# Four chained sequence layers on one core: layer-norm sums over chunks made on VectorE, the value bias of layer 3 moved behind the attention, and other load and product orders on both sides of attention 2

## The reference

```python
# layer 0: recurrent mixing with a token shift, then a small feed-forward part
xn = layernorm(x) * w + b;  dx = shifted(xn) - xn;  five mixes of xn and dx -> key, decay, value, receptance, gate
scan over the sequence (16 x 16 state per head), group norm, gate, @ Wo.T, + x
xn = layernorm(x) * w + b;  x = x + sigmoid(.. @ Wr.T) * (relu(.. @ Wk.T)**2 @ Wv.T)
# layer 1: cross attention of x on layernorm(context), 16 heads;  x = x + tanh(gate) * (attn @ Wo.T)
# layer 2: grouped cross attention, 32 heads on 8 key/value heads, bias on q, k, v, output;  x = layernorm(attn @ Wo + bo + x)
# layer 3 (x: context, latents: output of layer 2)
h = concatenate([x, latents], axis=1)
q = (latents @ q_w + q_b);  kv = (h @ kv_w + kv_b);  k, v = kv[..., 0], kv[..., 1]
attn = softmax(where(mask, q k^T / DH, -inf));  attn_out = attn @ v
attn_out = attn_out @ out_w + out_b + latents
out = rmsnorm(attn_out, postnorm_w);  out = gelu(out @ mlp_w1 + mlp_b1) @ mlp_w2 + mlp_b2;  return out + latents
```

## Time and profile before

| | us |
|---|---|
| median of three runs (lowest, highest) | 6026.17 (6018.28, 6046.16) |
| the profiled execution's own time | 6028.71 |
| its span in the profile | 6026.9 |
| TensorE busy | 5352.1 (89%) |
| VectorE busy | 3558.0 (59%) |
| ScalarE busy | 2765.7 (46%) |
| GpSimd busy | 1470.6 (24%) |

### The profile page before, as it was taken

How to read it: one execution, slowest core, us unless ns; L and a number is a source line. 1 busy time by engine, 2 the same in 40 slices (tenths; PEclk the granted TensorE clock), 3 DMA queues, 4 the chain that set the end, 5 groups by cost and what they waited for, 6 DMA issues and landing times. The chain is left out here.

```text
span 6026.9 us, 69068 instructions
## 1 busy us (share of the span) xinstructions
PE 5352.1 (89%) x26050; PEld 1878.7 (31%) x26050; DVE 3558.0 (59%) x4608; ACT 2765.7 (46%) x5261; POOL 1470.6 (24%) x708
## 2 busy tenths in 40 slices
PE   6987999999697999996788888886879999997999
PEld 2333333434233233322222222222323333322444
DVE  4548777877342777750588888881137777761010
ACT  2423333333122466662377777773215666663111
POOL 0004333334000466660000000000005666662000
PEclk8988999999799899998799999998979999998999
DMA  3233333333221322313111111112234232302000
GB/s 107 96 103 103 96 84 87 91 95 88 82 70 38 80 63 62 73 31 110 42 28 30 32 29 28 30 22 85 75 77 80 53 71 58 66 26 98 21 21 14
DMA packets 459769, 383.48 MB, mean 64 GB/s; under 512 B 169809, under 2 KB 359094, under 8 KB 458764
## 3 DMA queue, kind: packets, MB, share of 16 engines
q1 hardware_dynamic: 459428, 379.00, 23.4%
HBM read 242.83 MB, written 135.14 MB: 63 GB/s over the span
## 5 line engine op out<-in xcount | busy, mean ns | idle before, releaser
L2174 DVE TENSOR_REDUCE att_part<-att_scores 128x1 f32<-128x423 f32 (+1 forms) x2304 | 1190.2, 579 | 425.9 <-PE att_scores L2021 424.6
L2138 ACT ACTIVATE att_prob<-att_scores 128x512 f32<-128x512 f32 (+1 forms) x1920 | 993.5, 601 | 549.1 <-PE att_scores L2033 548.6
L2157 POOL TENSOR_TENSOR att_acc<-att_acc,att_prob 128x1024 f32<-128x1024 f32 (+1 forms) x416 | 984.7, 2367 | 441.3 <-ACT att_prob L2138 439.2
L2481 DVE TENSOR_REDUCE att_part<-att_scores 128x2 f32<-128x802 f32 x1024 | 964.6, 988 | 161.9 <-PE att_scores L2385 155.7
L2467 ACT ACTIVATE att_prob<-att_scores 128x512 f32<-128x512 f32 (+1 forms) x1664 | 861.4, 602 | 252.2 <-PE att_scores L2399 250.4
L2021 PE MATMUL att_scores<-att_k,att_q 97*128 97x423 f16 (+1 forms) x2304 | 816.5, 358 | 84.4 <-DMA att_q<-in_c_q 60.4
L2033 PE MATMUL att_scores<-att_q,att_k 98*128 98x512 f16 (+1 forms) x1920 | 721.5, 383 | 13.6 <-ACT att_prob L2138 13.4
L1264 POOL TENSOR_TENSOR scan_z<-scan_r,scan_states 128x512 f32<-128x512 f32 x256 | 410.1, 1602 | 1107.8 <-DVE scan_states L1297 1092.7
L2157 POOL TENSOR_TENSOR att_acc<-att_prob 128x1024 f32<-128x1024 f32 x32 | 75.6, 2364 | 2443.2 <-ACT att_prob L2138 2443.2
L2399 PE MATMUL att_scores<-att_q,att_k 49*128 49x512 f16 (+1 forms) x1664 | 471.7, 390 | 110.1 <-ACT att_prob L2467 109.9
L2044 PE MATMUL att_sums<-att_prob,att_v 128*32 128x512 f32 (+1 forms) x3840 | 510.9, 604 | 0.0
(11 more groups left out here) (294 smaller groups left out, 6103.3 us busy)
## 6 DMA issues: line engine op xcount, KB each, us to landing
v<-scan_val SPq DMA_DIRECT2D x96, 256.0 KB, 2.3
att_v<-v SPq DMA_DIRECT2D x32, 768.0 KB
att_spread<-recips SPq DMA_DIRECT2D x64, 256.0 KB
mix_plane<-in_mask SPq DMA_DIRECT2D x16, 800.5 KB, 6.6
att_k<-k1hi SPq DMA_DIRECT2D x32, 400.2 KB
att_k<-k3hi SPq DMA_DIRECT2D x32, 400.2 KB
scan_x<-in_ctx_t SPq DMA_DIRECT2D x12, 1024.0 KB, 8.9
o<-att_out SPq DMA_DIRECT2D x32, 256.0 KB, 2.1
```

The source lines that it names most:

```text
L2138: nc.scalar.activation(prob[g % NP][0:kw(kt), h, :], scores2[0:kw(kt), n % RING2, :], ACT.Exp).then_inc(exped, 1)
L2157: nc.gpsimd.tensor_tensor(acc[s % 2][0:kw(kt)], so_far[0:kw(kt), 0:PH, :], prob[g % NP][0:kw(kt), 0:PH, :], ALU.add).then_inc(padded, 1)
L2174: nc.vector.reduce_max(part[q % 2][:, hc, piece:piece + 1], scores1[:, bank["piece", p], 0:PIECE], AX.X).then_inc(reduced, 1)
L2481: nc.vector.reduce_max(part[q % 2][:, :, ec, piece], scores1[:, bank["unit", p], :, 0:PIECE], AX.X).then_inc(reduced, 1)
```

## The change

Six edits. In the four norm stages VectorE first adds the four chunks of x, or of `sq`, into `sq[:, 0]` (two adds, of 128 x 1024 and of 128 x 512), and the group on TensorE has one matmul instead of four. In "mlp" there is only the second moment. In "mix" VectorE adds up x when it comes to "mean" in its own order, and the squares behind that step's mask reductions.

```diff
@@ mix; ffn and mid2 the same, behind the residual add and behind the centring @@
                     if what == "mean":
-                        pe.wait_ge(xloaded[b % 2], 16 * (b // 2 + 1))
-                        group([(k["mean"][:], x[b % 2][:, c, :]) for c in range(C)])
+                        pe.wait_ge(totalled, 2 * b + 1)
+                        group([(k["mean"][:], sq[:, 0, :])])
                     elif what == "std":
-                        pe.wait_ge(squared, b + 1)
-                        group([(k["mean"][:], sq[:, c, :]) for c in range(C)])
+                        pe.wait_ge(totalled, 2 * b + 2)
+                        group([(k["mean"][:], sq[:, 0, :])])
...
+                def total_chunks(of):
+                    link(nc.vector.tensor_tensor(sq[:, 0:2, :], of[:, 0:2, :], of[:, 2:C, :], ALU.add))
+                    nc.vector.tensor_tensor(sq[:, 0, :], sq[:, 0, :], sq[:, 1, :], ALU.add).then_inc(totalled, 1)
...
                     if what == "mean":
+                        dve.wait_ge(xloaded[b % 2], 16 * (b // 2 + 1))
+                        total_chunks(xb)
                         dve.wait_ge(drained, ends[b, "mean"])
...
+                    if what == "mean":
+                        dve.wait_ge(squared, b + 1)
+                        total_chunks(sq)
```

The value bias of layer 3 leaves the value products of "scan" (two matmuls a group) and of "mid2" (one a group), with its loads and halves, and ScalarE adds it to the output of attention 3:

```diff
@@ scan @@
                         elif what == "v3":
-                            value_group(t, "v_w3", xs, m, rows["v_b3"])
+                            value_group(t, "v_w3", xs, m)
@@ att3, SP: ahead of load_keys(2) @@
+                if latents:
+                    for c in range(C):
+                        sp.dma_start(bias[:, c:c + 1], w["v_b3"][c * P:(c + 1) * P].unsqueeze(1)).then_inc(biased, 16)
@@ att3, ACT @@
+                def add_bias(s):
+                    act.wait_ge(weighed, s + 1)
+                    if s == 0:
+                        act.wait_ge(biased, 16 * C)
+                    nc.scalar.activation(out[s % 2][:], out[s % 2][:], ACT.Identity, bias=bias[:, s % C:s % C + 1]).then_inc(normed, 1)
...
+                    if kt == 14 and s and latents:
+                        add_bias(s - 1)
                     for h in range(QUAD):
...
+                if latents:
+                    add_bias(N - 1)
@@ att3, DVE @@
-                    nc.vector.tensor_tensor(out[i][:], sums_sb[i][:], spread[:], ALU.mult).then_inc(normed, 1)
+                    nc.vector.tensor_tensor(out[i][:], sums_sb[i][:], spread[:], ALU.mult).then_inc(weighed if latents else normed, 1)
```

In "mid1" o and x have four buffers each, and all loads are issued at the start. In "mid2" the key product is cut in two halves and the value product comes last:

```diff
@@ mid1, SP @@
                 def load(b):
-                    if b >= 2:
-                        sp.wait_ge(product, ends["out", b - 2])
-                    sp.dma_start(o[b % 2][:], rows_of(w["o1"], b)).then_inc(oloaded[b % 2], 16)
...
+                    sp.dma_start(o[b][:], rows_of(w["o1"], b)).then_inc(oloaded[b], 16)
+                    sp.dma_start(x[b][:], rows_of(w["x1"], b)).then_inc(xloaded[b], 16)
...
-                load(1)
+                for b in range(1, B):
+                    load(b)
                 store(0)
                 for b in range(B):
                     if b + 1 < B:
                         store(b + 1)
                     store_query(b)
-                    if b + 2 < B:
-                        load(b + 2)
@@ mid2, order @@
                 yield "query", b
                 if b + 1 < B:
                     yield "out", b + 1
-                yield "key", b
+                yield "key", b, range(0, C // 2)
                 if b + 1 < B:
                     yield "mean", b + 1
-                yield "value", b
+                yield "key", b, range(C // 2, C)
                 if b + 1 < B:
                     yield "std", b + 1
+                yield "value", b
@@ mid2, ACT: the second half of the key product @@
+                        if part[0].stop == C:
+                            act.wait_ge(drained, ends["key", b])
+                            if b:
+                                act.wait_ge(kstored, 32 * b)
+                            nc.scalar.activation(hi[1][:], q[:], ACT.Identity).then_inc(rounded, 1)
@@ mlp @@
                     elif what == "std":
-                        pe.wait_ge(squared, b + 1)
-                        group([(k["mean"][:], sq[:, c, :]) for c in range(C)])
+                        pe.wait_ge(totalled, b + 1)
+                        group([(k["mean"][:], sq[:, 0, :])])
```

More of the change, by code:

```diff
@@ L640, in _ @@
                     elif what == "mean":
-                        pe.wait_ge(residual, b + 1)
-                        group([(k["mean"][:], x[b % 2][:, c, :]) for c in range(C)])
+                        pe.wait_ge(totalled, 2 * b + 1)
+                        group([(k["mean"][:], sq[:, 0, :])])
                     elif what == "std":
-                        pe.wait_ge(squared, b + 1)
-                        group([(k["mean"][:], sq[:, c, :]) for c in range(C)])
+                        pe.wait_ge(totalled, 2 * b + 2)
+                        group([(k["mean"][:], sq[:, 0, :])])
                     elif what == "key":
@@ L905, in scan_and_keys @@
                "k_b3": ph.sb("bk3", [P, C])}
[L906 to L907 removed]
+        row = {"bv2": ph.sb("bv2", [1, P])}
+        rows = {"bv2": Halves(ph.sb("bv2h", [1, P], F16), ph.sb("bv2l", [1, P], F16))}
         one = ph.sb("one", [1, P], F16)
@@ L2636, in _ @@
                         for i in range(C):
-                            group([(W["Wq2"][:, c, i * P:(i + 1) * P], x[b % 2][:, c, :]) for c in range(C)])
+                            group([(W["Wq2"][:, c, i * P:(i + 1) * P], x[b][:, c, :]) for c in range(C)])
             @block.scalar
@@ L2706, in order @@
                     yield "out", b + 1
-                yield "key", b
+                yield "key", b, range(0, C // 2)
                 if b + 1 < B:
                     yield "mean", b + 1
-                yield "value", b
+                yield "key", b, range(C // 2, C)
                 if b + 1 < B:
                     yield "std", b + 1
+                yield "value", b
         ends, count = {}, 0
-        for what, b in order():
-            count += 1 if what in ("mean", "std") else C
+        for what, b, *part in order():
+            count += 1 if what in ("mean", "std") else len(part[0]) if part else C
             ends[what, b] = count
@@ L2776, in _, with project @@
                 group = Banks(nc, pe, psum, product, drained)
-                def project(b, weight, src):
+                def project(b, weight, src, part=range(C)):
                     if b == 0:
                         pe.wait_ge(wloaded[weight], 16)
-                    for i in range(C):
+                    for i in part:
                         group([(W[weight][:, c, i * P:(i + 1) * P], src[:, c, :]) for c in range(C)])
-                for what, b in order():
+                for what, b, *part in order():
                     if what == "out":
@@ L2788, in _ @@
                     elif what == "mean":
-                        pe.wait_ge(residual, b + 1)
-                        group([(k["mean"][:], x[:, c, :]) for c in range(C)])
+                        pe.wait_ge(totalled, 2 * b + 1)
+                        group([(k["mean"][:], sq[:, 0, :])])
                     elif what == "std":
-                        pe.wait_ge(squared, b + 1)
-                        group([(k["mean"][:], sq[:, c, :]) for c in range(C)])
+                        pe.wait_ge(totalled, 2 * b + 2)
+                        group([(k["mean"][:], sq[:, 0, :])])
                     elif what == "query":
@@ L2801, in _ @@
                             pe.wait_ge(wloaded["v_w3"], 16)
-                            pe.wait_ge(small, 16 * (len(vec) + 1))
                         for i in range(C):
-                            group([(x3[b % 2][:, c, i * P:(i + 1) * P], W["v_w3"][:, c, :]) for c in range(C)]
-                                  + [(k["ones"][0:1, :], bv[:])])
+                            group([(x3[b % 2][:, c, i * P:(i + 1) * P], W["v_w3"][:, c, :]) for c in range(C)])
             @block.scalar
@@ L2809, in _ @@
                 drain = Drains(nc, act, psum, product, drained)
-                act.wait_ge(small, 16 * (len(vec) + 1))
+                act.wait_ge(small, 16 * len(vec))
                 nc.scalar.activation(vec["q_b3"][:], vec["q_b3"][:], ACT.Identity, scale=1.0 / 32).then_inc(prescaled, 1)
                 act.wait_ge(prescaled, 1)
-                for what, b in order():
+                for what, b, *part in order():
                     if what == "out":
@@ L2849, in _, with total_chunks @@
                 link = Chain(dve, step)
-                dve.wait_ge(small, 16 * (len(vec) + 1))
-                for what, b in order():
-                    if what == "value":
+                def total_chunks(of):
+                    link(nc.vector.tensor_tensor(sq[:, 0:2, :], of[:, 0:2, :], of[:, 2:C, :], ALU.add))
```

(4 more changed lines are left out.)

80 lines of the change are left out of this document (42 added, 38 removed).

## The result

The changed kernel takes 5876.3 us (median of 4 runs, 5874.8 to 5910.9), the kernel before beside it on the same chip 6025.1 (6018.3 to 6046.2). The ratio is 0.976, 95% interval 0.973 to 0.978: 2.4% faster. The profiled execution took 5874.8 us with a span of 5873.0; the forecast was 5874.

A forecast was written before the change was run, and what follows sets the result against it. TensorE was taken to set the end nearly everywhere, by its own work or by being kept waiting. Terms 69.5 + 32.4 + 25 + 28.4 - 0.7 = 154.6 us off 6028.7 gave 5874; 8-in-10 range 5857 to 5912.

The forecast's parts named there:

- mid2: Stage mid2: new order hides the 8.5 us normalisation waits, with shorter statistics and no bias matmuls; gain 69.5 us, bounds 50-72.
- The 2 us to spare: mid2: normalisation ends about 12.5 us after std starts, std and value product cover 14.6, so 2 us remain.
- The rival of a normalisation that isn't hidden: mid2: each period keeps half its 8.5 us wait and its cold restart, 21 us less gain, 5895; chance 0.08.
- theory B: Run with only mid2's new order: four-matmul std uses up the spare 2 us, waits of 1 us and more stay.
- mid1: Stage mid1: two waits for loads of o, 13.47 and 13.23 us, go with their restarts; gain 32.4 us, bounds 26-33.
- scan: Stage scan: TensorE no longer runs single-row bias matmuls for 52 groups; gain 25 us, bounds 8-32.
- Statistics: mix, ffn and mlp: one matmul per statistic instead of four gains 12.7, 6.6 and 9.1, together 28.4 us; bounds 18-33.
- the price of 2.57: A statistic with one matmul instead of four frees 2.57 us of TensorE where it has other work meanwhile.
- the cooling rival: Added waits before statistics and "lora" make some seven places restart at lower clock, about 3 us each: 20 us, 5894; chance 0.06.
- att3: Stage att3: sixteen added ScalarE bias adds fit into idle time in 15 turns, the last costs 0.7 us; total -0.7.
- The slower-than-before rival: att3: ScalarE waits at tile 14 for VectorE's product, late from a DRAM broadcast; 15 us late gives 6044; chance 0.02.
- The rival on record: Changed kernel's rerun: att2's 8.5 us is a gain from unbroken mid1's warmer start; att2 again 1200.0 within 1 us.

The follow-up runs named there:

- the early add and the out product first: Changed kernel with att3's bias add ahead of ScalarE's waits, mid2's batch 1 out product ahead of batch 0's query: 5885.1 us; side by side 5861.8, ratio 0.972.

## Why the prediction was right, and where it was not

**mid2 (69.5 forecast, 68.4 measured).** The parts, each undone by itself: order 31.1, statistics 18.2, bias 20.0, together 69.3. The chain that I laid under the value product (last key drain, rounding, std drain, inversion, multiply, scale) was covered with no idle time in either kernel with the new order. The 2 us to spare were right too. VectorE's last scaling ahead of the third query ends at 4198.10, and that query starts at 4200.28, 2.2 us later:

```profile
4196.18 1.92 DVE L2899 TENSOR_SCALAR mid_x<-mid_y,mid_gamma,mid_beta 128x512 f32<-128x512 f32 x4
```

The rival of a normalisation that isn't hidden is out. A std of four matmuls does not use this time up, contrary to what I expected under theory B: the value product stands behind it, so a longer std puts the query off by as much as the chain. In the kernel with only the new order 9.3 us are left (4240.91 to 4250.17), since the bias rows lengthen the value product as well (18.6 for 13.7 us).

**mid1 (32.4; 31.7).** Undoing the edit brings back the two waits and 31.9 us. Shown.

**scan (25; 25.2).** Putting the bias rows back costs 22.6 us of stage in one profile; across all profiles with and without them scan lay at 1080.3 to 1084.1 against 1054.1 to 1061.1. The waits on ScalarE stayed (29.7 before, 29.5 after), so nothing was given back there. The gap itself closed: where 808.87 - 808.03 = 0.84 us stood between a v3 group and the mean, the changed kernel has 0.21:

```profile
790.81 0.38 PE L1084 MATMUL scan_psum<-scan_v_w3l,scan_xh 128*128 128x512 f16 x1
791.03 0.38 PE L1084 MATMUL scan_psum<-scan_v_w3h,scan_xl 128*128 128x512 f16 x1
791.24 3.60 PE L1084 MATMUL scan_psum<-scan_x,const_mean 128*128 128x512 f32 x8
```

The Trainium skill, Perfetto Trace Analysis, section Identifying the Most-Contended Engine, would have the weight loads tell how much headroom TensorE has (401 of 1058 us here, 38%). Read as slack of TensorE in scan, that is not what the runs show. For what sets the stage's time, start-to-start times of neighbouring matmuls were the better guide here.

**Statistics (28.4; 27.2 between the two profiles, some 23 over all of them).** The means over the three profiles with four matmuls and the nine with one differ by 9.4 in mix, 4.9 in ffn and 9.1 in mlp. The term was mis-sized where TensorE waits. mlp's 9.1 held, and so did the price of 2.57 where the statistic stands behind other work. In ffn I had read that TensorE waits for both statistics of a batch. Behind batch 0 it waited only for the std; the mean's price of 0.7 came out all the same (0.75), since the adds made TensorE wait. I priced each statistic at 0.7 as if it ran warm; with 3.57 us of idle time in front of it, the std ran at 1.94 instead of 1.13 us, and the batch shown gained 0.6 instead of 1.5. That is the cooling rival in small: it was right about the place, and cost under 1 us a batch here and not 3. The Trainium skill, TensorE: Matmul & The Clock Gate, section HAM oscillation, says that a gap between bursts is paid for at the restart; the trace agrees: it shows such a price behind 3.57 us of idle time (1.94 us), and none behind 1.56 us (1.13). Batch 0 of ffn has a part in the 6.0 us too that is not the change: its key product starts 83.8 us into the stage in before, 81.1 with four matmuls in the changed kernel, and 80.3 in the changed kernel. From 30 to 40 us into the stage before had a granted clock of 0.50, the others 0.54 to 0.62.

In mix two places fell short of the 12.7. VectorE's first add starts at 25.01, behind its wait for a small load (mix_prev), while TensorE could start on x at 23.63 before; so batch 0's mean ends 0.6 us earlier (1.1 against the kernel with four matmuls) where I had 2. And the "lora" product of batch 2 took 7.25 us behind 3.43 us of idle time in all three profiles with four matmuls, and 9.12 behind 7.70 in the changed kernel (8.8 to 9.1 behind 4.9 to 7.7 in all nine with one): 1.9 us for the restart. The idle times in front of "lora" of batches 1 to 3 were 6.1, 7.7 and 7.7 us, for the 7 to 8 forecast.

**att3 (-0.7; -7.0): the step that failed.** The prediction said "So the bias add fits into the idle time in 15 turns". It fitted by length, 0.7 in 1.95 us, but not by place. The idle time was itself a wait, for PE's counts of an earlier tile, and in ScalarE's program the add stands behind that wait. So it ran when the exponentials could have run, and delayed most turns by 0.25 us (58.62 to 58.87). Fifteen turns make 4.5 us (865.9 to 870.4 from the first drain to the last). The end costs 1.4 (16.2 to 17.6 from the last drain). Of that the add has 0.75: the last store is issued 1.47 us after VectorE's product starts, where it was 0.72 (5475.16 to 5475.88), and I had 0.7:

```profile
5330.00 0.69 DVE L2227 TENSOR_TENSOR att_out<-att_sums_sb,att_spread 128x512 f32<-128x512 f32 x1 [6.61 <-DMA att_spread<-recips]
5330.73 0.72 ACT L2135 ACTIVATE att_out<-att_out,att_bias 128x512 f32<-128x512 f32 x1 [9.84 <-DVE att_out L2227]
5331.47 0.32 SPq L1977 DMA_DIRECT2D o<-att_out  x1
```

The rest is a wait for the spread inverse of 6.61 us where it was 6.11, and 4.8 us for 4.6 from the store to the next stage; why is open. The start costs 0.9 (131.9 to 132.8), which did not repeat in the later runs (131.1 to 132.4), so it is not put down to the change. The experiment with the add ahead of the wait gives the turns back but for 0.7 us (866.6), so the cause is shown. The slower-than-before rival, a late VectorE product, looked at the wrong wait: VectorE was in time.

**att2 (0; +8.5).** Not a gain. The prediction had no term for it, and the range of 5857 to 5912 would have held a run with the long form too, if closely (5910.9 occurred). Without that luck the sum would have been some 8 us off. Nearly all of it arises in two places, some 3 us at the first and 7 at the second, with a little given back elsewhere. 60 to 70 us into att2 the granted clock was 0.53 in before and 0.99 in after, and 560 us into it before has this stretch at the lower level, with TensorE busy throughout, and after has none:

```profile
3468.00:3478.00 10.00, 10.00 (x45) 1.98 (x41) 5.90 (x7) 4.77 (x10) 0.00 (x0) 0.50 0.00 0
3478.00:3488.00 10.00, 10.00 (x50) 2.04 (x51) 6.61 (x8) 5.55 (x11) 0.00 (x0) 0.59 0.01 2
```

The kernel with the early add has the changed kernel's short mid1 and chunk totals, and in its profile both are there again (0.50 at 60 us, 0.53 from 520 to 540 us) with 1208.6 us. The rival on record, that the unbroken mid1 lets att2 start warmer, falls too: the kernel with the bias in the products has the short mid1 and 0.50 at 60 us, the one with only mid2's order has the long mid1 and 0.95. And the changed kernel itself took 1200.0, 1200.4 and 1223.2 us in its three profiles. So it is not the change.

## What to carry to other kernels

Before putting an instruction into an engine's idle time, look at which wait makes that time, and put it ahead of that wait in the engine's program; behind it, it is not in the gap but on the path. An order that places a long independent product behind the last statistic hid the normalisation whole in mid2. The first batches of ffn and mlp still wait in the same way (9.4 us before ffn's key product, 7.1 before mlp's statistic); no run tried to fill these. An add that frees an engine elsewhere can itself stand behind an unrelated wait, as in mix. And when a sum comes out exact, compare stage by stage: here two errors of 8.5 and 6.3 us had cancelled.

## What the hardware showed that I had not expected

att2 is the same code in all kernels, and yet lies between 1198 and 1234 us. The records tell where. In all profiles the granted clock is at the lower level (0.50, 1.2 of 2.4 GHz) in the stage's first 60 us, and then at full level for most of its length, with short falls at places that differ. The long stretch does not differ in place. In five of the ten later profiles the clock falls 1135 to 1147 us into the stage, where VectorE has nearly all of its work behind it, and stays at 0.50 until about TensorE's last product. Two kernels at this place, first the one with only mid2's order, then the one with the early add and the out product first (window, then the columns of the stage table); each shows the 5 us ahead of it and what follows:

```profile
4036.00:4041.00 5.00, 3.20 (x25) 0.81 (x26) 3.86 (x6) 3.17 (x7) 0.00 (x0) 1.00 0.02 3
4041.00:4110.00 69.00, 61.75 (x228) 8.24 (x220) 1.64 (x3) 37.52 (x73) 0.00 (x0) 0.53 0.04 12
```

```profile
3962.00:3967.00 5.00, 3.20 (x25) 0.81 (x26) 3.83 (x6) 3.17 (x7) 0.00 (x0) 1.00 0.02 2
3967.00:4012.00 45.00, 35.43 (x228) 8.07 (x220) 1.64 (x3) 37.35 (x73) 0.00 (x0) 1.00 0.07 19
```

The same 228 matmul records keep TensorE busy for 61.75 us at a granted clock of 0.53 and for 35.43 at 1.00. The profiles with such a stretch lie 20 to 33 us above 1200 (the longest has other falls too). The unprofiled runs spread by as much, which fits, but only profiles show where. What decides whether the clock falls stays open. TensorE is a little less busy right ahead of it, 3.20 of 5 us, but that is so in both kernels shown, and the stretch appeared with and without each edit of the change. No run tried to provoke it.
